# Router logits of a fused attention and mixture-of-experts layer: from expert-major to token-major matmuls, with two scale steps, one store and one statistics step moved

## Time and profile before

| | |
|---|---|
| runs, us | 2776.94, 2776.83, 2775.22 |
| the profiled execution, us | 2776.94 |
| its span on the core, us | 2775.2 |
| PE, busy us and share | 2734.5, 99% |
| DVE | 2179.6, 79% |
| ACT | 1407.4, 51% |
| POOL | 646.2, 23% |
| mean granted PE clock | 0.994 |

### The profile page before, as it was taken

One profiled execution on the slowest core, in us unless ns is written; L12 is line 12 of the kernel. 1 busy time (PEld: TensorE's weight loads), 2 busy tenths in 40 slices (PEclk: granted clock), 3 DMA queues, 4 the chain that ended last, 5 costly groups with the idle time before them and its releaser, 6 DMA issues.

```text
span 2775.2 us, 41671 instructions
## 1 busy us (share of the span) xinstructions
PE 2734.5 (99%) x13008; PEld 2265.7 (82%) x13008; DVE 2179.6 (79%) x3165; ACT 1407.4 (51%) x2500; POOL 646.2 (23%) x658
## 2 busy tenths in 40 slices
PE   8999999999999999999999999999999989999998
PEld 7888888888888888888888888888887777888877
DVE  5888888888888888888888888888888778533346
ACT  5555555566555555655555557555554432244434
POOL 2121122122211221222222213111121110356520
PEclk9999999999999999999999999999999999999999
DMA  3111111113111111221111111211110231388953
GB/s 118 38 35 38 34 34 35 37 34 110 34 36 39 34 34 38 65 80 34 36 36 34 36 40 57 87 34 34 34 49 12 93 111 42 107 245 251 249 158 137
DMA packets 209638, 193.50 MB, mean 70 GB/s; under 512 B 14620, under 2 KB 162076, under 8 KB 209552
## 3 DMA queue, kind: packets, MB, share of 16 engines
q1 hardware_dynamic: 199056, 180.47, 20.5%
q0 software_dynamic: 10496, 12.02, 2.3%
HBM read 166.41 MB, written 36.18 MB: 73 GB/s over the span
## 4 chain that ended last, share of the span: by engine, by line
PE 89%; DVE 4%; DMA 3%; issue 2%; ACT 1%; POOL 0%; POOLq 0%; ACTq 0%; DVEq 0%; SPq 0%
PE banks L1719 37%; PE banks L1734 24%; PE banks L1757 12%; PE banks L1641 5%; PE banks L1690 3%; PE banks L1650 3%; DMA acc_rows<-rows_b,who 3%; PE banks L1744 2%; PE banks L1703 2%; DVE colsum L1279 1%; PE banks L1566 0%; POOL acc_rows L689 0%; PE banks L1677 0%; DVE neg_max L1264 0%; ACT rows_b L854 0%
## 5 line engine op out<-in xcount | busy, mean ns | idle before, releaser
L1719 PE MATMUL banks<-xt,w_sb 128*128 (+1 forms) x4608 | 1108.0, 389 | 6.4 <-DVE xt L1358 6.4
L915 ACT ACTIVATE rows_a<-banks,neg_max 128x1024 f32<-128x1024 f32 x512 | 572.5, 1118 | 893.0 <-DVE neg_max L1264 892.7
L1719 PEld LDWEIGHTS banks<-xt,w_sb 128*128 128x128 f32 x4608 | 866.2, 188 | 186.4 <-POOL w_sb L628 6.3
L1264 DVE TENSOR_REDUCE neg_max<-banks 128x1 f32<-128x1024 f32 x512 | 625.7, 1222 | 286.3 <-PE banks L1734 283.3
L1734 PE MATMUL banks<-qk 128*128 128x512 f32 x3072 | 780.9, 390 | 3.3 <-ACT rows_a L915 3.3
L1734 PEld LDWEIGHTS banks<-qk 128*128 128x128 f32 x3072 | 576.9, 188 | 124.9 <-issue 3.4
L1279 DVE SCALAR_TENSOR_TENSOR colsum<-rows_a,inv,colsum 128x1024 f32<-128x1024 f32 x448 | 586.3, 1309 | 18.8 <-DVE inv L1271 1.5
L628 POOL TENSOR_TENSOR w_sb<-raws,w_sb 128x512 fp32r<-128x512 f32 x192 | 258.0, 1344 | 1200.6 <-ACT w_sb L869 1200.6
L1757 PE MATMUL banks<-wo_sb,val 128*128 128x512 f32 x1536 | 372.1, 391 | 1.2 <-DVE y_sb L1314 1.2
L1757 PEld LDWEIGHTS banks<-wo_sb,val 128*128 128x128 f32 x1536 | 285.9, 188 | 67.8 <-DVE y_sb L1314 8.0
L633 POOL TENSOR_TENSOR wo_sb<-wo_raw,wo_sb 128x512 fp32r<-128x512 f32 x64 | 95.9, 1499 | 415.3 <-ACT wo_sb L875 415.3
(11 more groups left out here) (180 smaller groups left out, 2293.3 us busy)
## 6 DMA issues: line engine op xcount, KB each, us to landing
raws<-in_w_qkv SPq DMA_DIRECT2D x192, 256.0 KB, 2.8
wo_raw<-in_w_o SPq DMA_DIRECT2D x64, 256.0 KB, 2.8
y_sb<-in_x SPq DMA_DIRECT2D x32, 256.0 KB, 3.7
raw_own<-in_w_gate SPq DMA_DIRECT2D x16, 512.0 KB, 4.8
raw_own<-in_w_up SPq DMA_DIRECT2D x16, 512.0 KB, 5.2
raw_own<-in_w_down SPq DMA_DIRECT2D x16, 512.0 KB, 6.6
raws<-in_xT SPq DMA_DIRECT2D x25, 256.0 KB, 3.0
x_wide<-y_sb SPq DMA_DIRECT2D x24, 256.0 KB, 3.6
```

Source lines behind the costliest of these rows:

```text
L915: act.activation(ex[:, t % 2], p_s[:, t % 2], ACT.Exp, bias=neg_max[:, t % 2], accum_out=rowsum[:, t % 2]).then_inc(act_e, 1)
L1264: dve.tensor_reduce(neg_max[:, t % 2], p_s[:, t % 2], AX_X, ALU.max, negate=True)\
L1719: ins = pe.matmul(p_g[:, g % 2], w_sb[:, a, r, c], xt_part(batch_par, b, c, half * NB, NB), start=(c == 0 and (a, b) == PASSES[0]), stop=( ...
```

## The change

- `logits(c)` of an early turn now has the tokens as the stationary operand. For each of 4 tiles and 4 chunks it issues two matmuls: HI part of the tokens against 64 columns (HI and LO of the router's weights side by side), and LO part against 32 columns, 32 matmuls in all. `copy_l`, `logit_rows`, `logit_T` and `twice` are gone; `gate_up` runs unbroken.
- `add_logits(c)` on DVE adds the two halves from PSUM into `logit`; `sigmoid_r` of an early turn reads `logit` and waits for it. For turn 0 `sigmoid_r` stands two instructions earlier on ACT.
- `scale_x(6)` and `scale_x(7)` move from POOL to DVE, in the form that `scale_o` has (12 instructions): the first ahead of `weigh(0)`, the second behind `collect(2)`.
- On SP `store_x(7)` now stands ahead of `load_rows(5)`.
- On DVE `stats_o(0)` now stands ahead of `share_step(5, 1)` instead of behind `lo_t(3, 1)`.

```diff
@@ SP
         load_rows(4)
+        store_x(7)
         sp.wait_ge(pe_t, TT * 4)
         load_rows(5)
-        store_x(7)
         store_a(2)
@@ POOL
-        scale_x(6)
...
-            if c == 1:
-                scale_x(7)
@@ ACT
         def sigmoid_r(c):
             on_act.wait_ge(dve_w, 2 * c)
-            on_act.wait_ge(pe_r, c + 1)
-            act.activation(prob[:], p_r[:, :, 0], ACT.Sigmoid).then_inc(act_r, 1)
+            if split(c, False):
+                on_act.wait_ge(dve_l, share(c) + 1)
+                act.activation(prob[:], logit[:], ACT.Sigmoid).then_inc(act_r, 1)
...
-        copy_l(0)
+        sigmoid_r(0)
         hi_t(1, 2)
         hi_t(1, 3)
-        sigmoid_r(0)
@@ DVE
+        def scale_x(c):
+            on_dve.wait_ge(act_q, 2 * TT * (c + 1))
+            on_dve.wait_ge(act_ln, TT * (c - 1))
+            ln_rsqrt(dve, link, EPS, n_square[:, c % 2], small[:, 0], n_scale[:, c % 2], small[:, 2], 1.0 / D)
+            tt(n_shift[:, c % 2], n_mean[:, c % 2], n_scale[:, c % 2], ALU.mult).then_inc(scaled, 1)
+        def add_logits(c):
+            on_dve.wait_ge(pe_r, c + 1)
+            on_dve.wait_ge(act_r, c)
+            dve.tensor_reduce(logit[:], p_r.rearrange("p t a e -> p t e a"), AX_X, ALU.add).then_inc(dve_l, 1)
...
         lo_t(2, 3)
+        scale_x(6)
         weigh(0)
...
             collect(u)
-
+            if u == 2:
+                scale_x(7)
+
+        add_logits(6)
...
         share_step(5, 0)
+        stats_o(0)
         share_step(5, 1)
         lo_t(3, 0, True)
         lo_t(3, 1, True)
-        stats_o(0)
@@ PE
-                for part, k in ((HI, 0), (LO, 0), (LO, 1), (LO, 2), (LO, 3), (HI, 1), (HI, 2), (HI, 3)):
...
+                for j in range(TT):
+                    for k in range(KC):
+
+                        pe.matmul(p_r[:, j], x[:, HI, k, cols(j)], r_sb[:, k], start=(k == 0), stop=False)
+                        ins = pe.matmul(p_r[:, j, 0], x[:, LO, k, cols(j)], r_sb[:, k, HI], start=False,
+                                        stop=(k == KC - 1))
...
-        def logit_rows(c):
...
-            gate_up(n, 0, range(0, 12))
-            logit_rows(u)
-            gate_up(n, 0, range(12, 24))
+            gate_up(n, 0)
```

More of the change, by code:

```diff
@@ L259, in layer @@
     out_rows = [rows_c[:], y_sb[:, 0:TT], as_rows(xT_flat[:]), rows_a, rows_b[:], y_sb[:, TT:2 * TT]]
-    logit_T = sb("logit_T", [2 * E, NB])
-    twice = sb("twice", [2 * E, E])
+    logit = sb("logit", [P, TT, E])
     prob = sb("prob", [P, TT, E])
@@ L291, in layer @@
     p_r = psum[:, 6, 0:TT * 2 * E].rearrange("p (t a e) -> p t a e", t=TT, a=2)
-    p_l = psum[0:2 * E, 6]
     p_c = psum[:, 7]
@@ L323, in layer @@
     pe_t, act_t, dve_t = sem("pe_t"), sem("act_t"), sem("dve_t")
-    pe_r, pe_l, act_l, act_r = sem("pe_r"), sem("pe_l"), sem("act_l"), sem("act_r")
-    pool_tw = sem("pool_tw")
+    pe_r, dve_l, act_r = sem("pe_r"), sem("dve_l"), sem("act_r")
     dve_w, pe_c, dve_e = sem("dve_w"), sem("pe_c"), sem("dve_e")
@@ L712, in _ @@
         lo_wo(M - 1, 1)
-        pool.wait_ge(pe_o, T * PAIRS)
-        pool.tensor_tensor(twice[:], ident[0:2 * E, 0:E], ident[0:2 * E, E:2 * E], ALU.add).then_inc(pool_tw, 1)
         for h in range(2):
@@ L798, in sigmoid_r @@
             on_act.wait_ge(dve_w, 2 * c)
-            on_act.wait_ge(pe_r, c + 1)
-            act.activation(prob[:], p_r[:, :, 0], ACT.Sigmoid).then_inc(act_r, 1)
-        def copy_l(c):
-            on_act.wait_ge(pe_l, share(c) + 1)
-            on_act.wait_ge(pe_r, c)
-            act.copy(logit_T[:], p_l).then_inc(act_l, 1)
+            if split(c, False):
+                on_act.wait_ge(dve_l, share(c) + 1)
+                act.activation(prob[:], logit[:], ACT.Sigmoid).then_inc(act_r, 1)
+            else:
+                on_act.wait_ge(pe_r, c + 1)
+                act.activation(prob[:], p_r[:, :, 0], ACT.Sigmoid).then_inc(act_r, 1)
         def sigmoid(n, f):
@@ L1003, in _ @@
         for n, u in enumerate(EARLY[1:3], 1):
-            copy_l(u)
             sigmoid_r(u)
@@ L1022, in _ @@
                 write_x(7)
-        copy_l(6)
         sigmoid_r(6)
@@ L1031, in _ @@
         hidden(3, 2)
-        copy_l(7)
         sigmoid_r(7)
@@ L1387, in _ @@
         dve.wait_ge(in_b, 16)
+        add_logits(0)
         lo_t(2, 0)
@@ L1404, in _ @@
         for n, u in enumerate(EARLY[1:3], 1):
+            add_logits(u)
             choose_groups(u)
@@ L1447, in _ @@
         lo_hidden(3, 2)
+        add_logits(7)
         choose_groups(7)
@@ L1574, in logits @@
                 on_pe.wait_ge(dve_s, 1)
-            on_pe.wait_ge(act_r, c)
+            else:
+                if split(c - 1, False):
+                    on_pe.wait_ge(dve_l, share(c - 1) + 1)
+                else:
+                    on_pe.wait_ge(act_r, c)
             if split(c, False):
@@ L1578, in logits @@
                 x = parts[:, PARTS_OF[c]]
-                for part, k in ((HI, 0), (LO, 0), (LO, 1), (LO, 2), (LO, 3), (HI, 1), (HI, 2), (HI, 3)):
-                    if part == HI:
-                        ins = pe.matmul(p_l, r_sb[:, k].rearrange("p a e -> p (a e)"), x[:, HI, k],
-                                        start=(k == 0), stop=(k == KC - 1))
-                    else:
-                        pe.matmul(p_l[0:E], r_sb[:, k, HI], x[:, LO, k], start=False, stop=False)
-                ins.then_inc(pe_l, 1)
+                for j in range(TT):
[3 more added lines that the diff above has]
+                                        stop=(k == KC - 1))
             else:
@@ L1591, in logits @@
                                         start=(k == 0), stop=(k == KC - 1))
-                ins.then_inc(pe_r, 1)
-        def logit_rows(c):
-            on_pe.wait_ge(act_l, share(c) + 1)
-            on_pe.wait_ge(pool_tw, 1)
-            for j in range(TT):
-                ins = pe.matmul(p_r[:, j, 0], logit_T[:, cols(j)], twice[:], start=True, stop=True)
             ins.then_inc(pe_r, 1)
@@ L1812, in _ @@
         turn(1, 3)
-        logit_rows(0)
         turn(2, 0)
@@ L1846, in _ @@
             logits(u + 2)
-        gate_up(3, 0, range(0, 12))
-        logit_rows(6)
-        gate_up(3, 0, range(12, 24))
+        gate_up(3, 0)
         count(5)
@@ L1860, in _ @@
         count(6)
-        gate_up(3, 3, range(0, 12))
-        logit_rows(7)
-        gate_up(3, 3, range(12, 24))
+        gate_up(3, 3)
         down(3)
```

## The result

| | us |
|---|---|
| after, median of 4 executions (lowest to highest) | 2802.41 (2795.53 to 2803.43) |
| before, 4 executions on the same chip | 2776.02 (2771.47 to 2776.94) |
| ratio after to before | 1.0093 [1.0074, 1.0113] |
| a second measurement of the same two kernels | 2798.74 and 2776.68, ratio 1.0071 [1.0055, 1.0088] |
| the profiled execution after, and its span | 2804.82, 2803.1 |

The change makes the kernel slower: by 26.4 us between the medians of the first measurement and 22.1 in the second. The ratios give 25.8 and 19.7. The forecast was 16.9; the first median lies outside its range, the second inside it. It can differ from the difference of the medians by up to 3.2 us.

A forecast was written before the change was run, and what follows sets the result against it. PE's chain of waits was taken as the bound, with DVE setting the pace in routing up to `count(2)`. Terms 3.2 + 0.8 + 4.1 + 1.7 - 0.2 + 7.3 = 16.9 on 2776.94 gave 2793.8 us, range 2786 to 2801.

The forecast's parts named there:

- DVE's chain, +3.2: Routing up to `count(2)`: `scale_x(6)` and `add_logits` lengthen DVE's work without slack, reaching PE in full, +3.2 us.
- The new logits, +0.8 a turn: Where PE is the bound: 32 matmuls at 115 ns cost +1.8 us, dropping `logit_rows` saves 1.0, +0.8 a turn.
- the 3.7 us of turn 1 lost no clock: Argument against more low clock: turn 1's router matmuls, a stretch of small matmuls, ran 3.7 us without a clock loss.
- Turn 5's rows, +4.1: At `turn(5, 0)`: PE waits for `load_rows(5)`, queued behind `store_x(7)`, which waits for `write_x(7)` and `scale_x(7)`; +4.1 us.
- The clock after that wait, +1.7: Behind PE's new wait for turn 5's rows: a lower granted clock costs +1.7 us, from 0 to 1.7.
- the old fall at 2300: Window 2300 to 2304 of the profile before, behind `fill`, `logits` and `count`: clock at 0.58, 1.7 us lost.
- The rest of routing, -0.2: Turns 6 and 7: turn 6 costs 0.8 us again, the removed `logit_rows(7)` gives 1.0 back; -0.2 us.
- The tail, +7.3: DVE stops for the `stats_o(0)` fetch, PE waits 10.4 us at `turn(3, 2)`, `down(5)` starts 9.0 later; +7.3 us.
- the old wait: Tail of the profile before: PE waits 3.3 us for DVE ahead of `down(5)`; its lower clock, 1.7 us, was subtracted.
- more low clock or slower logits: Rival in routing: up to two more clock falls, 3.4 us, or 193 ns matmuls; about 2797.2 us, chance 0.20.

The follow-up runs named there:

- the change with the sixteen matmuls: Kernel after, plus 16 overwritten matmuls of 512 columns where PE waits for `rows_a`, ahead of `turn(5, 0)`: ratio 1.0072 to the kernel before, median 2795.68 us.
- the split logits on the kernel before: Kernel before with only the new logits, those of turns 2, 4, 6 and 7 placed between two halves of a `gate_up`: ratio 1.0030.
- the second profile after: The kernel after once more, unchanged, profiled in an execution of 2804.26 us.
- the second profile before: The kernel before once more, unchanged, profiled in an execution of 2770.86 us.
- the one with both statistics late: Kernel before with only `stats_o(0)` and `stats_o(2)` moved behind `share_step(5, 3)`: ratio 0.9995.

## Why the prediction missed

1. **DVE's chain, +3.2: hidden behind the half clock.** Its parts are there (`scale_x` 2.35 us, `add_logits` 0.42), but in every profile with the long early fall PE reaches `count(2)` 6.2 to 6.8 us later against the start of the stage, scale steps or not. Where that fall was short the term shows: `count(2)` was 4.8 and 3.8 us late with the scale steps (the change without the moved store, and the change with the sixteen matmuls), DVE waited for nothing in front of `scale_x(6)`, and it was 1.7 us late without them (the split logits on the kernel before).
2. **The new logits, +0.8 a turn: the step that failed.** The pace was right, 111 ns against 115. The clock that such a stream brings on was put in a rival, set aside with "the 3.7 us of turn 1 lost no clock". That took one execution's reading for a property of the place: the new logits of turn 0, ahead of those 3.7 us, make the half clock common there (8 of 11 profiles against 1 of 6; by the mean clock 7 of 11 executions against 11 of 92). Alone, turn 0 costs 5.6 us and the other four 6.4; all five together cost 3.9 by their ratio and 8.4 in the routing stage of their profile. The forecast's part for them was about 1.5 in all. The bounds of this term came from durations alone, so the range had no room for it.
3. **Turn 5's rows, +4.1: right**, 3.7 us, by the path named. The load landed 8.5 us after its issue, where 7.2 were worked out, and it was issued 4.4 us later than forecast. PE came 6.1 us later too. The two delays nearly cancel in the wait, so the nearness of its size is in part luck.
4. **The clock after that wait, +1.7: right in kind.** The windows 2296 to 2304 stand at 0.50 and 0.75, 3.0 us lost; filling the wait gave 2.9 back. In exchange the old fall at 2300 is gone in this profile, which the prediction kept; in the second profile after it is back (`gate_up` of 24 matmuls behind it 7.05 us, against 5.72).
5. **The rest of routing, -0.2: wrong by the same cause as 2**, 3.0 us at turn 6 (`fill(4)` to `count(5)` +3.8, forecast +0.8). That too varies from one execution to the next: of the eleven profiles with the new logits of turn 6 unsplit, this stretch is 3.8 us longer in five, 2.2 in three (the second profile after among them) and 0.6 in three.
6. **The tail, +7.3: right in kind, near in size partly by luck.** From the start of turn 5's shared expert to the end the profile has 7.15, and alone the move cost 9.2 us by its ratio (10.9 between the medians). But the exchange for the old wait rests on one execution: against the second profile before the same stretch has 12.3.

The sum of what was missing in the profile, 11.0 us: 0.8 in attention, 3.3 up to `count(2)`, 0.4 to `fill(2)`, 2.1 at turn 4 with the wait, -1.5 to `fill(4)`, 3.0 at turn 6, 0.2 to the experts, 2.9 in the routed experts, -0.15 in the tail. The experts' 2.9 is not the change's: the second profile after has -0.6 there and the second before -0.6. The experiments leave open why the early fall comes in one execution and not in the next, and why, once begun, it lasts over 13 us; nor was the store's move tried on the kernel before alone, or turn 0's new matmuls without their `add_logits` and earlier sigmoid.

The rival "more low clock or slower logits" was the true one. It was given 0.20 and 3.4 us; in the profile low clock in routing grew by 14.5 us, of which 3 stand behind the wait that term 4 priced at 1.7. How much of the rest fell on time that PE would have waited anyway was not worked out.

## What to carry to other kernels

Price a change of matmul shapes twice: by the spacing of the matmuls, and by the granted clock of the dense work behind them; here 8 long matmuls swapped for 32 short ones, next to other short ones, were followed by the half clock with no wait of PE in front. Compare PE's busy time over the whole stage and (1 - clock) times its length before looking for new waits. And take no slack, wait or fall of one profile as fixed: the second profile of the unchanged kernel showed that the tail's old wait, part of term 6, was one execution's.

## What the runs showed of the hardware

- At full clock, 32 matmuls with a new 128 x 128 stationary operand each and 64 or 32 moving columns in turn start 111 ns apart, and at half clock 213 ns; 64 or 32 columns made no difference.
- The half clock of 2200 to 2213 covered, in every profile that had it, the same work, and lasted 13 to 14 us; the other stretches at 0.50 in the windows above lasted 3 to 7 us. Of the profiles with nothing added ahead of it, eight of eleven with the new logits in turn 0 had it, and one of six with the old ones there. The other three of the eleven had a short fall in its place (0.57 in the window 2204 to 2208; one of them also 0.50 from 2198 to 2200); the other five of the six stand at 1.00 in every window from 2200 to 2212.
- Executions of the one unchanged kernel before ranged from 2770.9 to 2786.5 us, roughly in line with its mean granted clock (0.996 to 0.991). The same routing program took 213.8 us in one profile and 221.1 in another (the one with both statistics late), so a difference of two profiles under about 7 us says little about a change.
